# The prologue of a gated cross-attention and FFN kernel: writes on ScalarE's queue, a transposition moved, side work placed elsewhere

## The reference

```
x = x + tanh(g_x) * attention(layernorm(x), ctx, ctx)      # 32 heads of 16, 8 groups of keys and values
x = x + tanh(g_f) * (shared_mlp(h) + routed_mlp(h) * w),   h = layernorm(x)
attention: q = h Wq', k = ctx Wk', v = ctx Wv';  softmax(q k' / 4) v;  then Wfc' and bias bfc
mlp: (silu(h G') * (h U')) D';  shared 2048 wide, routed 256 wide;  w = sum of the softmax of the two best router logits
```

## Time and profile before

| | |
|---|---|
| profiled execution | 890.05 us, span 887.7 us |
| three plain runs | 887.41, 887.93, 888.95 us |
| busy, share of the span | PE 97%, PE weight loads 72%, VectorE 72%, ScalarE 38%, GpSimd 54% |
| chain that ended last | PE 84%, VectorE 11%, issue 2%, ScalarE 1%, DMA 1% |
| DMA | 71.88 MB, mean 81 GB/s |

### The profile page before, as it was taken

One profiled execution on the slowest core, in us unless ns is written; L12 is line 12 of the kernel. 1 busy time (PEld: TensorE's weight loads), 2 busy tenths in 40 slices (PEclk: granted clock), 3 DMA queues, 4 the chain that ended last, 5 costly groups with the idle time before them and its releaser, 6 DMA issues.

```text
span 887.7 us, 14887 instructions
## 1 busy us (share of the span) xinstructions
PE 860.1 (97%) x4923; PEld 642.5 (72%) x4923; DVE 635.8 (72%) x1085; ACT 337.2 (38%) x636; POOL 477.8 (54%) x485
## 2 busy tenths in 40 slices
PE   8689999999999889999999999999999999999998
PEld 6445665665565447888888888888788888888886
DVE  7789899889889966666556655679665566656565
ACT  4186576667657852122112211344211121112111
POOL 2313004001203999787668666954966696678640
PEclk9889999999999999999999999999999999999999
DMA  7763342432432113121112111211311112111102
GB/s 274 232 175 105 127 121 61 149 116 78 131 107 74 38 28 93 48 72 47 47 47 71 47 47 47 72 47 65 115 59 48 47 52 66 47 47 47 47 1 95
DMA packets 43609, 71.88 MB, mean 81 GB/s; under 512 B 6064, under 2 KB 21936, under 8 KB 43312
## 3 DMA queue, kind: packets, MB, share of 16 engines
q1 hardware_dynamic: 43568, 71.34, 25.5%
HBM read 55.33 MB, written 15.73 MB: 80 GB/s over the span
## 4 chain that ended last, share of the span: by engine, by line
PE 84%; DVE 11%; issue 2%; ACT 1%; DMA 1%; SPq 0%; DVEq 0%; ACTq 0%
PE bank L1293 24%; PE bank L1295 23%; PE bank L1294 23%; DVE mcol L906 5%; PE bank L1353 4%; PE bank L1378 4%; PE bank L1368 3%; PE bank L1298 2%; PE bank L1399 1%; DVE oN L1038 1%; ACT probs L761 1%; DVE oB L1028 1%; DVE x_l L1256 1%; DVE aT_l L881 0%; DMA q_scr<-qx_l 0%
## 5 line engine op out<-in xcount | busy, mean ns | idle before, releaser
L1293 PE MATMUL bank<-x_l,w_h 128*128 128x512 f32 x504 | 197.3, 391 | 0.3 <-DVE c L1116 0.3
L1294 PE MATMUL bank<-x_h,w_l 128*128 128x512 f32 x504 | 196.2, 389 | 0.0
L1295 PE MATMUL bank<-x_h,w_h 128*128 128x512 f32 x504 | 196.2, 389 | 0.0
L906 DVE TENSOR_REDUCE mcol<-bank 128x2 f32<-128x512 f32 x256 | 164.7, 671 | 24.8 <-PE bank L1353 24.3
L620 ACT ACTIVATE hT_h<-bank 128x512 fp32r<-128x512 f32 x72 | 43.1, 599 | 355.9 <-DVE bank L1231 347.2
L761 ACT ACTIVATE probs<-bank 128x512 f32<-128x512 f32 x256 | 138.9, 596 | 73.3 <-PE bank L1368 71.7
L572 POOL TENSOR_TENSOR w_l<-raw,w_h 128x512 fp32r<-128x512 f32 (+1 forms) x144 | 161.9, 1157 | 2.9
L1128 DVE SCALAR_TENSOR_TENSOR xa<-bank,tgf,xa 128x512 f32<-128x512 f32 x128 | 96.2, 751 | 77.7 <-PE bank L1295 77.5
L1293 PE MATMUL bank<-dn_l,hT_h 128*128 128x512 f32 x288 | 112.0, 389 | 0.0
L1294 PE MATMUL bank<-dn_h,hT_l 128*128 128x512 f32 x288 | 112.0, 389 | 0.0
L1295 PE MATMUL bank<-dn_h,hT_h 128*128 128x512 f32 x288 | 112.0, 389 | 0.0
(11 more groups left out here) (149 smaller groups left out, 1340.6 us busy)
## 6 DMA issues: line engine op xcount, KB each, us to landing
raw<-w_gu SPq DMA_DIRECT2D x36, 512.0 KB, 3.3
dnraw<-w_dn SPq DMA_DIRECT2D x36, 256.0 KB, 2.6
q_st<-q_scr SPq DMA_DIRECT2D x64, 128.0 KB, 2.7
q_scr<-qx_h SPq DMA_DIRECT2D x16, 256.0 KB, 2.2
q_scr<-qx_l SPq DMA_DIRECT2D x16, 256.0 KB, 2.2
q_st<-q_scr SPq DMA_DIRECT2D x64, 64.0 KB, 2.7
out<-xa SPq DMA_DIRECT2D x16, 256.0 KB, 2.0
cx_raw<-ctxT SPq DMA_DIRECT2D x14, 256.0 KB, 3.0
```

The lines of the kernel that those rows point to most:

```text
L906: v.tensor_reduce(at[:, :, qt], sm_bank(n, s, u)[:, :].rearrange("p (r k) -> p r k", r=2), AX.X, ALU.max).then_inc(max_ok, 1)
L1293: mm(out, a_h, b_l, start=start, stop=False, skip_group_check=onto)
L1294: mm(out, a_l, b_h, start=False, stop=False, skip_group_check=onto)
L1295: return mm(out, a_h, b_h, start=False, stop=stop, skip_group_check=onto)
```

## The change

On SP the load of the last block of x moves from step 0 to behind the other two, ahead of bias, gates and router weight, and the writes of block 0's k and q go. ScalarE issues them instead, after its own copies (`first_k`, `first_q`). VectorE takes k's low half ahead of the second half of Wq's, all statistics in the prologue, and its `wfc_low` and aggregates later. TensorE forms both transpositions of v of block 0 in the prologue, transposes the first maxima behind the second pair of score 1, and issues 22 matmuls of 128x512 whose result nobody uses (`bridge`). GpSimd's last roots and block 1's bias sums move from step 4 to step 5.

```diff
@@ -338,7 +338,7 @@
             sp.dma_start(wq_raw, wq).then_inc(in_wq, 16)
-            for t in (1, 2):
+            for t in range(1, BLOCKS):
                 sp.dma_start(xa[:, TILES * t:TILES * (t + 1), :], x_v[t]).then_inc(in_x[t], 16)
@@ -346,15 +346,9 @@
             sp.wait_ge(warm, 1)
-            write_k(0)
-            write_q(0, 0)
             read_k(0, 0)
-            read_q(0, 0, 0, 0, True)
-            write_q(0, 1)
-            write_q(0, 2)
-            read_q(0, 0, 1, 0, True)
-            write_q(0, 3)
-            read_q(0, 0, 2, 0, True)
+            for c in range(3):
+                read_q(0, 0, c, 0, True)
             put_max(0, 0)
@@ -378,8 +372,6 @@
                         sp.dma_start(raw0[:, A11:, :].rearrange("p a k -> p (a k)"), w_gu[0, :, :]).then_inc(in_gu[0], 16)
-                    if s == 0 and first:
-                        sp.dma_start(xa[:, T // P - TILES:T // P, :], x_v[BLOCKS - 1]).then_inc(in_x[BLOCKS - 1], 16)
                     if s == 4 and not last:
@@ -489,9 +481,9 @@
                         cx_low(t + 1, s)
-                    if first and s == 4:
+                    if first and s == 5:
                         deviations(2)
-                    if s == 4:
+                    if s == (5 if first else 4):
                         add_bias(t + 1)
@@ -707,16 +699,38 @@
             x_high(0, 3)
+            def first_k():
...
+                act.wait_ge(consts, CONSTS)
+                act.wait_ge(warm, 1)
+                act.wait_ge(k_hi, 1)
+                for part in range(2):
+                    nc.scalar.dma_start(k_scr[0, :, part, :], kx_h[:, :].bitcast(f32)).then_inc(k_wr, 16)
+                act.wait_ge(k_lo, 1)
+                nc.scalar.dma_start(kl_scr[0, :, :], kx_l[:, :].bitcast(f32)).then_inc(kl_wr, 16)
...
+            def first_q(oc):
...
+                for part, (done, tile) in enumerate(((q_hi, qx_h), (q_lo, qx_l))):
+                    act.wait_ge(done, oc + 1)
+                    nc.scalar.dma_start(q_scr[0, oc, :, part, :], tile[:, oc % 2, :].bitcast(f32)).then_inc(q_wr[oc], 16)
...
             v_copy(0)
+            first_k()
             act.wait_ge(in_vectors, 64)
...
             q_high(0, 0)
+            first_q(0)
             q_high(0, 1)
+            first_q(1)
             q_high(0, 2)
+            first_q(2)
             vt_copy(0, 0)
+            vt_copy(0, 1)
             q_high(0, 3)
+            first_q(3)
             act.wait_ge(wq_ok, 2)
@@ -765,7 +779,7 @@
                             a_high(n - 1, (s - 1) % CHUNKS, (s - 1) % STEPS // CHUNKS, 2 * t + (s - 1) // CHUNKS)
-                        if (s, u) == ((0, 5) if last else (2, 3)):
+                        if not first and (s, u) == ((0, 5) if last else (2, 3)):
                             vt_copy(t, 1)
@@ -984,21 +998,23 @@
             x_low(0, 3)
+            k_low(0)
             wq_low(1)
-            k_low(0)
             dve.wait_ge(in_x[1], 16)
-            for i in range(TILES, TILES + 2):
+            for i in range(TILES, TILES + 3):
                 tile_stats(i)
...
             v.tensor_scalar(tbias[:, :], tbias[:, :], tgx[:, :], None, ALU.mult).then_inc(tb_ok, 1)
-            for i in range(TILES + 2, 2 * TILES):
+            tile_stats(TILES + 3)
+            dve.wait_ge(in_x[2], 16)
+            tile_stats(2 * TILES)
+            q_low(0, 1)
+            for i in range(2 * TILES + 1, 3 * TILES):
                 tile_stats(i)
-            q_low(0, 1)
-            dve.wait_ge(in_x[2], 16)
-            for i in range(2 * TILES, 3 * TILES):
-                if i == 2 * TILES + 2:
-                    q_low(0, 2)
+            q_low(0, 2)
+            dve.wait_ge(in_x[BLOCKS - 1], 16)
+            for i in range(3 * TILES, 4 * TILES):
                 tile_stats(i)
@@ -1054,14 +1070,11 @@
-                        if first and s in (2, 3) and u == 6:
-                            wfc_low(s - 2)
-                        if first and s in (2, 3) and u in (4, 7):
-                            dve.wait_ge(in_x[BLOCKS - 1], 16)
-                            tile_stats(T // P - TILES + 2 * (s - 2) + u // 7)
-                        if first and s == 4 and u == 0:
+                        if first and (s, u) in ((3, 6), (5, 4)):
+                            wfc_low(s // 4)
+                        if first and s == 5 and u == 0:
                             aggregates(BLOCKS - 1)
-                        if first and s == 5 and u == 0:
+                        if first and s == 6 and u == 0:
                             norm_rows(2)
@@ -1072,6 +1085,8 @@
                             if u == 7:
+                                if first and s == 5:
+                                    dve.wait_ge(wfc_ok, 2)
                                 a_low(n - 1, (s - 1) % CHUNKS, (s - 1) % STEPS // CHUNKS)
@@ -1399,6 +1414,13 @@
+            def bridge(count):
...
+                for _ in range(count):
+                    mm(PJ[1][:, :], wq_h[:, 0, 0:P], wq_h[:, 0, :], start=True, stop=True)
...
+            WARM = (2, 0, 3, 3, 3, 2, 1, 2, 2)
             pe.wait_ge(consts, CONSTS)
@@ -1427,17 +1449,24 @@
             vt_job(0, 0)
+            pe.wait_ge(k_lo, 1)
+            vt_job(0, 1)
             pe.wait_ge(q_lo, 2)
             q_job(3)
+            pe.wait_ge(vt_cp, 2)
+            bridge(WARM[0])
             pe.wait_ge(k_rd[0], 64)
...
                 sm_pair(0, 0, v, 0, 0)
-            pe.wait_ge(q_lo, 3)
-            mt_job(0, 0)
+                bridge(WARM[1 + v])
             pe.wait_ge(q_rd[1], 64)
...
                 sm_pair(1, 1, v, 0, 1)
+                bridge(WARM[5 + v])
+                if v == 1:
+                    pe.wait_ge(q_lo, 3)
+                    mt_job(0, 0)
             pe.wait_ge(q_lo, CHUNKS)
@@ -1458,6 +1487,8 @@
                         st_pair(n, v, bb, c)
+                        if first and s == 0 and v in (0, 2):
+                            bridge(2)
                         if v == 0 and not (first and s == 0):
@@ -1541,7 +1572,7 @@
                             if first:
-                                pe.wait_ge(k_lo, 1)
+                                pe.wait_ge(vt_cp, 2)
                             else:
@@ -1553,7 +1584,8 @@
                             pe.wait_ge(x_lo, TILES * nx + 4)
-                            vt_job(t, 1)
+                            if not first:
+                                vt_job(t, 1)
                         if s == 2 and v == 3:
```

## The result

The changed kernel is slower: median 893.82 us of 20 runs (887.94 to 896.20) against 889.03 of 20 runs of the kernel before on the same chips (887.41 to 891.05), ratio 1.0039 [1.0027, 1.0051]. The forecast was 883.4, the range 881.3 to 886.3. Its times fall into two groups: eight from 887.9 to 891.7, twelve from 893.1 to 896.2. The profiled execution (895.75 us, span 893.9) is one of the second; a later profile of the same kernel (e12) caught one of the first. The forecast started from 887.93, the median of three runs; the twenty put the kernel before at 889.03, so 1.1 us of the miss is that base.

What follows compares the result with a forecast made beforehand. TensorE, busy 97% of the span, was taken as the bound, with only the beginning movable. Gains 0.55 + 1.28 - 0.15 + 1.9 + 0.88 = 4.46 us gave 883.4 us, range 881.3 to 886.3.

Steps and rivals of the forecast that it cites:

- I take it that it stays at 2.4 GHz here: First two scores: with bridges TensorE is busy 0.71 of the time, so its clock was taken to stay full.
- Rival D: Clock falls before or at the first score, bridges become the bound in scores and step 0: 890.5 us, slower; chance 0.05.
- Step 0's 1.9: Step 0: at full clock, with ScalarE setting the pace, it gets shorter by 1.9 us (1.0 to 2.4).
- ScalarE's 8.50 of 8.50 us, unchanged: Step 1: ScalarE is busy throughout, so the length up to its later start was taken not to change.
- The start: Prologue: writes on ScalarE's queue and statistics moved ahead bring the first maximum 0.55 us sooner (-0.15 to +1.15).
- The Trainium skill: Writes by ScalarE: rule that several issuing engines save only initiation time; by it the sum would be 884.0 us.
- Transposing between later scores: Two scores: score 1's first pairs go ahead of the first maxima's transposition, closing VectorE's hole; gain 1.28 us (0.9 to 1.28).
- The 0.15 for the maxima's DMA: Start of step 0: the maxima reach the queue later, so TensorE waits for their DMA; loss 0.15 us (0 to 0.6).
- Step 4: VectorE work taken out of steps 2 and 3 removes TensorE's wait for a maximum there; gain 0.88 us (0 to 1.3).
- Step 2: VectorE work leaves it only after TensorE's idleness has passed, so nothing is gained: 0.
- E: Rival: more than TensorE's idle 0.88 us goes, step 2 also starts without VectorE's lag; 881.8 us, chance 0.11.
- Step 5: wfc_low and aggregates, 1.4 us, fit VectorE's free 1.46 us: nothing, or 0.4 if they fall before a needed maximum.

Runs made afterwards that it cites:

- e12: The changed kernel once more, unaltered, run for a profile of its lower group; 889.15 us, span 887.3.
- e1: The changed kernel without any of its 22 bridge matmuls; 889.51 us, ratio 1.0003 to the kernel before.
- e8: The changed kernel with 14 bridges ahead of the first score and more behind the pairs of scores; 889.89 us, ratio 1.0012 to the kernel before.
- e15: The changed kernel, bridges in, with only block 0's writes of k and q back on SP in the old order; 888.62 us, ratio 0.9997.
- e7: The changed kernel without bridges, with the second wfc_low at unit 7 of step 4 instead of unit 4 of step 5; 888.06 us, ratio 0.9999.
- e9: The changed kernel with 6 bridges ahead of the first score, more behind the pairs, and the second wfc_low in step 4; 888.09 us, ratio 0.9990.
- e5: The changed kernel without bridges, with q2's write held until q0's read has landed; 888.97 us, ratio 1.0011 to the kernel before.
- e6: The changed kernel without bridges, with SP's reads of q1 held until q0's read has landed; 889.97 us, ratio 1.0014 to the kernel before.
- e13: The changed kernel, bridges in, with q2's write held until q0's read has landed; 889.89 us, ratio 1.0012, 4 of 12 runs above 892 us.
- e14: The changed kernel, bridges in, with SP's reads of q1 held until q0's read has landed; 891.12 us, ratio 1.0032, 5 of 12 runs above 892.
- e16: The changed kernel, bridges in, with both q2's write and q1's reads held until q0's read has landed; 888.99 us, ratio 1.0011.
- e3: The kernel before with only the bridge matmuls added, same places and number; 890.22 us, ratio 1.0017.
- e4: The kernel before with only the transposition of the first maxima moved behind the second pair of score 1; 888.07 us, ratio 0.9993.
- e10: The changed kernel without bridges, block 0's writes back on SP, the second wfc_low in step 4; 887.06 us, ratio 0.9980 to the kernel before.
- e11: As e10, with 4 bridges ahead of the first score, more behind the pairs and the four of step 0; 887.58 us, ratio 0.9989.
- e2: The changed kernel with 14 bridges instead of 2 ahead of the first score; 5 runs from 888.97 to 894.77 us, ratio 1.0047.

## Why the prediction was wrong, point by point

**The failed step is "I take it that it stays at 2.4 GHz here".** Rival D is what happened, and it stood at 0.05. Its point of decision was right (the clock fell at 34.4 us, 0.1 ahead of the first score), and so nearly was its price for the scores: three bridges in 1.58 us (I had 3 x 0.46), a loss of 4.3 against VectorE's pace where I had 3.4. Its time, 890.5, was 3.3 low: 1.1 is the base, and the start and step 5 also went the other way. The stretch that I leaned on, 64 to 66 us with TensorE busy 0.54 of it, had no such wait ahead of it: from 53.5 to 66 us TensorE never waited longer than 0.92 us in one piece, here 2.64. The reason given against D, two bridges in the gap, did not hold: they ended 2.64 us before the read. The other one, step 0 nearly full at half clock just before the clock came back, was no help either: TensorE was busy 14.61 of 14.61 and 10.28 of 10.32 us, and the clock came back only at 58.3 us. e1 (10.32 us without bridges), e12 (10.32 with them at full clock) and the changed profile (14.61) show the mechanism. Between the two executions of one program the price is 6.6 us of span, 1.2 of it the read itself; 12 of 20 executions lay in the upper group.

**Step 0's 1.9 was right for a clock that held and wrong as a gain of the program.** e8 has 1.83 in step 0 and gives 0.85 back in step 1, 0.36 of it more work of ScalarE's and 0.49 ScalarE's wait behind the maxima's DMA; "ScalarE's 8.50 of 8.50 us, unchanged" was the error. In the changed profile both steps lost.

**The start: 0.55 sooner forecast, 1.94 later measured** (0.73 in e12, 0.85 in e1). q0's copy ran at 22.77, not 23.7 (at 23.07 in e12, where it stood behind w_r): 1 MB more ahead of w_r cost only what the queue took. But the write took 4.15 us where I had 2.6, and the read 4.66 from its last issue where I had 2.9:

```profile
22.77 0.60 ACT L612 ACTIVATE qx_h<-bank 128x512 fp32r<-128x512 f32 x1 [0.17 <-PE bank L1310]
...
24.13 0.57 ACTq L716 DMA_DIRECT2D q_scr<-qx_l  x1
```

The DMAs issued from 21 to 34 us, with the median time from issue to landing, after and in e15:

```profile
q_scr<-qx_l ACTq DMA_DIRECT2D x3, 256.0 KB, 4.2
q_st<-q_scr SPq DMA_DIRECT2D x4, 128.0 KB, 3.5
```

```profile
q_scr<-qx_l SPq DMA_DIRECT2D x3, 256.0 KB, 3.5
q_st<-q_scr SPq DMA_DIRECT2D x3, 128.0 KB, 3.1
```

In these two profiles writes by the second queue land 0.7 us later and reads beside them 0.4 (in the kernel before the same two medians are 3.9 and 2.8). Over the profiles whose chain shows q0's read, one execution each: with moved writes it takes 3.44 to 4.66 us (the changed kernel, e1, e7, e9, e12), with a hold 2.92 to 3.45 (e5, e6, e13, e14, e16), with the writes on SP 2.72 to 2.90 (the kernel before, e3, e4). So SP's order, which kept q1's and q2's writes behind q0's read, was a priority and not a loss, and nobody had waited for the 3.4 us by which I read q1's write as late.

q0's low write is another matter. It takes 3.51 to 4.45 us in the same ten profiles with moved writes, held or not, and my 2.6 in e15 and 2.5 in e10 (with SP's writes and k's low half late, 3.10 in e3, 3.17 in e4 and 4.25 in the kernel before). In e15 k's reads are issued behind it (25.42 against 24.58 us), in the changed kernel ahead of it (23.28 against 24.13); no run holds k's reads, so whether they are what lengthens the write was not tested.

The Trainium skill (DMA: Bandwidth & Descriptors, section Issuing engines are not separate DMA queues), which the prediction weighed and set aside, came out right in that nothing was gained by it: with the writes back on SP, e15 starts its first score 1.05 us before e12, and e10 0.2 before e7.

Not settled: why executions above 892 us are frequent with bridges and moved writes together (26 of 56, over the changed kernel, e13, e14 and e16), against 2 of 32 with bridges and the writes on SP (e15, e11, and e3's 892.19) and none of 40 with the moved writes and no bridges (e1, e5, e6, e7); with more bridges it is 3 of 27 (e2, e8, e9). Neither hold ended them, though in e14 and e16's profiles the read was early; of each kernel's upper group one trace at most was seen, so how many of them come by the late read and how many by the second fall stays open.

**Transposing between later scores: right.** 1.28 forecast; e4 shows 1.38 in the two scores, 1.26 by step 6 and about 1.0 in the median (888.07 against 889.10 beside it, not clear of noise by its interval). The 0.15 for the maxima's DMA was not needed: in the traces of e4, e1 and e8 TensorE does not wait for it at step 0. Where step 0 runs at full clock it waits at step 1 instead, for the second score's: 1.11 us in e8, 1.32 in e14, 1.38 in e11.

**Step 4: right,** 0.88 forecast, 0.78 measured in the changed profile and in e1 and e10 alike. Step 2, forecast 0, gave 0.77 in the changed profile, 0.34 in e1 and 0.01 in e10: it follows where TensorE and ScalarE stand, as E said it might.

**Step 5: mis-sized.** Forecast 0, or 0.4 if the work fell before a needed maximum; measured 1.20 in the profile, of which e7 against e1 wins back 0.95. VectorE had 1.46 us free for 1.4 us of work, but the piece of 1.22 takes 2.10 beside GpSimd's sums, which the change had moved into the same step. I had timed each move on its own.

**What adds up for the lower group:** in e12 the start (+0.73), the scores (-1.46), step 0 (+0.27), step 1 (+0.23), step 2 (-0.34), step 3 (-0.08), step 4 (-0.77) and step 5 (+1.19) leave -0.23 at step 6, and the span is 0.4 below that of before. Even without D the change was worth little, because the losses at the start and in step 5 eat the gains of the transposition and of step 4. e10 keeps those two gains, with e7's place for the subtraction, and drops the writes' move and the bridges.

## What to carry to other kernels

Filler matmuls meant to hold the clock must be priced at the low clock first: if their sum with the real work then exceeds what the pacing engine leaves, they turn a harmless low clock into the bound, and a late transfer is enough for that. An order of transfers in one queue can be a priority; before moving them to a second queue, ask whose landing gets later, not whose issue gets sooner. A VectorE instruction with two SBUF inputs that is moved must be laid beside GpSimd's timetable.

## What was unexpected of the hardware

- The same program had its clock fall at 34.4 us in one profile and at 43.8 in another, 6.6 us apart in span; with fourteen bridges it did not fall at all in the profile taken, yet two of five runs were in the upper group.
- A TensorE that is busy without a gap does not have its clock back at once: in the changed profile it was full at 1.2 GHz for some 24 us, from 34.4 to 58.3; in e12 for some 7, from 43.8 to 50.7.
- In seven profiles, with bridges and without (the changed kernel's, e4, e6, e9, e13, e15, e16), the clock fell a second time between 58 and 68 us, for some 3 us in four of them and for 10 to 14 in e6, e15 and e16, and it does not take an idle TensorE just before: ahead of e4's fall at 61.8 us it was busy 1.96 of 2 us. The cost went from nothing (e4's step 2: 10.18 us) to nearly 3 (e6's and e15's: 12.95 and 12.96). What starts it was not found.
- Bridges did not always prevent the fall where they kept the clock up at first: in e11 and e14 it held until 54 us and then fell in step 1.
- A write of 256 KB from ScalarE's queue took 4.15 us in one execution and 3.56 in another; its issue took 0.34 to 0.57 us of ScalarE, near SP's 0.43.
